# Where in the turn of the interaction stage the small product, the relu rows and the normalising stand

## The reference

```
h  = relu(layernorm(x))
hidden = silu(attr8 @ Wfc1 / sqrt(8));  w = (hidden @ Wfc2 / 8) as 4 x 32 for each edge
xs1, xv1 = (scalar and vector part of h[src]) * node_attr_input[src] @ w1 / sqrt(32)
m0, m3, m1, m2 = products of w, xs1 or xv1 and edge_attr (1 scalar, 3 vector parts)
mid = segment_sum([m0 m3 m1 m2], dst) / 4
x3 = x2 + node_attr_output * (mid @ w2) / sqrt(64)
h  = relu(layernorm(x3));  base = x3 + h + bu'
n  = normalise(h);  ndT = (n * ln_g + ln_b) transposed;  attention terms = wa.T @ ndT
```

## Time and profile before

| | |
|---|---|
| median of 3 runs | 4488.05 us (4477.16 to 4498.65) |
| profiled execution, its own time | 4457.76 us |
| its span in the trace | 4456.1 us |
| PE, DVE, ACT, POOL busy | 3021.5, 3403.5, 2148.5, 2108.6 us |
| mean granted clock of PE | 0.819 |

### The profile page before, as it was taken

How to read it: one execution, slowest core, us unless ns; L and a number is a source line. 1 busy time by engine, 2 the same in 40 slices (tenths; PEclk the granted TensorE clock), 3 DMA queues, 4 the chain that set the end, 5 groups by cost and what they waited for, 6 DMA issues and landing times. The chain is left out here.

```text
span 4456.1 us, 67687 instructions
## 1 busy us (share of the span) xinstructions
PE 3021.5 (68%) x12366; PEld 1720.8 (39%) x12366; DVE 3403.5 (76%) x10033; ACT 2148.5 (48%) x5598; POOL 2108.6 (47%) x2258
## 2 busy tenths in 40 slices
PE   5956644444445999478999124888888999506886
PEld 1255533333332444123444112555545666303443
DVE  6978868888886888675555785888885666597997
ACT  0057766677662222162222265676765666304554
POOL 0057767777775554006553002555545555103566
PEclk9977767777767999689999555898888999758998
DMA  2079966776672222174331596444445556303333
GB/s 51 2 209 285 285 219 219 231 232 227 225 219 87 65 62 59 45 222 86 62 62 42 135 246 157 121 125 121 126 107 180 194 195 199 112 0 110 114 112 87
DMA packets 622136, 627.73 MB, mean 141 GB/s; under 512 B 168453, under 2 KB 495711, under 8 KB 615589
## 3 DMA queue, kind: packets, MB, share of 16 engines
q1 hardware_dynamic: 574020, 523.79, 39.3%
q0 software_dynamic: 48000, 102.76, 9.4%
HBM read 333.97 MB, written 296.91 MB: 142 GB/s over the span
## 5 line engine op out<-in xcount | busy, mean ns | idle before, releaser
L1410 PE MATMUL r_pM<-r_masked,wr 128*128 128x512 f32 x1600 | 747.3, 620 | 55.2 <-DVE r_masked L1361 55.2
L1361 DVE SCALAR_TENSOR_TENSOR r_masked<-r_typ,r_hT 128x512 f32<-128x512 f32 x800 | 493.9, 688 | 238.4 <-ACT r_hT L1388 189.1
L1410 PEld LDWEIGHTS r_pM<-r_masked,wr 128*128 128x128 f32 x1600 | 307.7, 198 | 424.3 <-issue 293.2
L1252 PE MATMUL e_pY<-ident,e_agg 128*128 128x128 f32 x400 | 134.0, 438 | 367.6 <-DVE e_agg L1127 340.3
L741 POOL DMA_INDIRECT q_rows<-nr,row_x x200 | 258.8, 1294 | 193.3 <-PE q_pT L590 132.3
L2408 POOL DMA_INDIRECT out<-o_base,o_at_o x200 | 239.4, 1197 | 165.1 <-DVE o_base L2449 96.8
L741 POOL DMA_INDIRECT r_xs<-h_tab,r_at_s x200 | 214.8, 1074 | 87.7 <-issue 47.0
L741 POOL DMA_INDIRECT r_xs<-tab,r_at_s x200 | 212.4, 1062 | 89.1 <-issue 48.2
L1252 PEld LDWEIGHTS e_pY<-ident,e_agg 128*128 128x128 f32 x400 | 106.9, 327 | 379.5 <-issue 202.4
L590 PE MATMUL g_pT<-ident,g_hT 128*128 128x128 f32 x400 | 95.9, 384 | 226.7 <-ACT g_hT L1772 176.0
L1006 PE MATMUL na_pZ<-w,na_aT 128*128 128x128 f32 x784 | 158.9, 385 | 117.5 <-ACT na_aT L988 117.4
(11 more groups left out here) (402 smaller groups left out, 8958.4 us busy)
## 6 DMA issues: line engine op xcount, KB each, us to landing
xz<-na_xz SPq DMA_DIRECT2D x49, 1040.0 KB, 5.7
r_typ<-vec_s SPq DMA_DIRECT2D x100, 256.0 KB, 3.4
g_al<-alpha_s SPq DMA_DIRECT2D x100, 256.0 KB, 4.3
na_xz<-in_x SPq DMA_DIRECT2D x49, 512.0 KB, 7.0
tab<-na_x SPq DMA_DIRECT2D x49, 512.0 KB
e_xin<-tab SPq DMA_DIRECT2D x49, 512.0 KB, 6.4
hr<-e_hh SPq DMA_DIRECT2D x49, 512.0 KB, 3.8
zh_s<-e_zh SPq DMA_DIRECT2D x49, 512.0 KB, 4.5
```

The costliest lines, as they stand in the source:

```text
L1252: pe.matmul(pY[s][:, cols], agg[s][:, cols], g.ident[:, :], start=True, stop=False)
L1361: v.scalar_tensor_tensor(masked[:, r, :], typ[d.slot(4)][:, :], float(r), hT[d.slot(2)][:, :], ALU.is_equal, ALU.mult).then_inc(ev.mk, 1)
L1410: pe.matmul(pM[s][:, :], g.wr[:, layer * R_ + r, :], masked[:, r, :], start=(r == 0), stop=(r == R_ - 1)).then_inc(ev.mm, 1)
```

## The change

`line = Line(4, 10, 8)` gives one turn more. On DVE the small product and the normalising leave the end of the turn and stand behind the scan and hid, now for blocks t-5 and t-6. On ACT the relu rows leave the end of the turn and stand between the copies hT and ws, for block t-5. What follows n (PE's transposes, ndT, product with wa, attention terms, the stores) goes one turn later. Statistics, rz, rh and POOL's adds keep their lags.

```
-    line = Line(4, 10, 7)
+    line = Line(4, 10, 8)
 sync:
-                b = at(6)   # store of n, then of base
+                b = at(6)   # store of base
+                b = at(7)   # store of n
-                b = at(7)   # stores of ndT, att
+                b = at(8)
 vector, behind hid (L1916) and ahead of the messages:
+                b = at(5)
+                if b:
+                    v.wait_ge(ev.rz, b.now())
+                    v.wait_ge(ev.hh, b.back(1))
+                    v.scalar_tensor_tensor(nm[:, :], mv[:, :, 0], -1.0, rz[:, :], ALU.mult, ALU.mult).then_inc(ev.nm, 1)
+                d = at(6)
+                if d:
+                    s = d.slot(2)
+                    v.wait_ge(ev.rh, d.now())
+                    v.wait_ge(ev.ts, d.back(2))
+                    if d.k >= 2:
+                        v.wait_ge(w_n[s], 16 * d.uses(2))
+                    normalise(v, hh[s], mvh, rh, n_[s], ev.nn)
 vector, at the end of the turn: the same lines for at(4) and at(5) are removed
 scalar, behind hT (L1999) and ahead of ws (L2002):
+                d = at(5)
+                if d:
+                    s = d.slot(2)
+                    a.wait_ge(ev.nm, d.now())
+                    a.wait_ge(ev.nn, d.back(2))
+                    a.wait_ge(ev.ba, d.back(2))
+                    for j in range(J):
+                        last = a.activation(hh[s][:, j, :], x3[s][:, j, :], ACT.Relu, scale=rz[:, j:j + 1], bias=nm[:, j:j + 1])
+                    last.then_inc(ev.hh, 1)
 scalar, at the end of the turn: the same lines for at(4) are removed
 scalar: ndT and att, both at(6) -> at(7)
 tensor: f = at(6) -> f = at(7)
```

More of the change, by code:

```diff
@@ L1856, in turn @@
                     s = b.slot(2)
-                    wait_alone(g, sp, ev.nn, b.now())
-                    sp.dma_start(b.edge_rows(g.nr, N), n_[s][:, :, :]).then_inc(w_n[s], 16)
                     wait_alone(g, sp, ev.ba, b.now())
@@ L1861, in turn @@
                 b = at(7)
+                if b:
+                    s = b.slot(2)
+                    wait_alone(g, sp, ev.nn, b.now())
+                    sp.dma_start(b.edge_rows(g.nr, N), n_[s][:, :, :]).then_inc(w_n[s], 16)
+                b = at(8)
                 if b:
@@ L1961, in turn @@
                     stats(v, c, g, hh[d.slot(2)], sth, mvh, ev.sh)
[L1962 to L1972, removed]
             line.sweep(v, turn, c)
@@ L2009, in turn @@
                     a.activation(sg[:, :], sg[:, :], ACT.Exp, scale=-1.0).then_inc(ev.si, 1)
-                b = at(6)
+                b = at(7)
                 if b:
@@ L2033, in turn @@
                     rstd(a, g, c, mvh, rh, ev.rh)
[L2034 to L2041, removed]
             line.sweep(a, turn, c)
@@ L2048, in turn @@
             def turn(at):
-                f = at(6)
+                f = at(7)
                 if f:
```

## The result

After: 4465.79 us in the median (4457.16 to 4471.82, 12 runs). Before, on the same chip: 4484.11 us (4470.82 to 4498.65, 12 runs). The ratio is 0.9964 (95% interval 0.9952 to 0.9975), some 16 us: a small gain that this many runs can tell from nothing. The two medians differ by 18.3 us. The forecast was 4473 and 15 us.

The account below looks back on a forecast made before the run. Neither DVE nor PE is full; waits inside an interaction turn bound it, DVE ending full-clock turns, PE slow-clock ones. 41 turns x (11.74 - 11.38) = 15 us saved, plus 1, less 1, carried from 4488.05 to 4473 us; range 4448 to 4501.

Parts of the forecast that it names:

- Path of a turn: In the interaction stage: scan, hid, small product, normalising, products, pM, ACT, pL, 11.31 us a turn at full clock.
- The hold: A DVE instruction with both operands in SBUF stands until 1.12 us after a POOL add has begun.
- lower end of 10.64: The interaction turn with nothing in the way of the products: 10.64 us.
- Rival (a): POOL's adds don't meet DVE's products; turn 10.64 to 10.75 us, 42 us saved, 4446 us; chance 0.17.
- The hold to the end of the instruction: DVE's products stand until each POOL add ends: 11.65 us a turn, kernel within 3 us of before.
- rival c: No change at all: DVE held to each POOL instruction's end, or short clock falls not hidden; 4485 to 4489; chance 0.12.
- The clock: PE's long falls, which make 12.97 us turns, go; a short fall in one turn of three costs 0.07 us a turn.
- Every turn ends with pL: PE's product pL ends every new turn, as in the 18 turns with no fall behind them, so long falls should go.
- Rival (b): Clock keeps falling for long in at least every second turn; 4505 us at one half, 4538 in all; chance 0.13.
- new stand before pM: PE waits 1.5 us each turn for the last message product before its transposes into pM.
- Sum: Interaction stage: 15 us saved in 41 turns, 1 us in four turns before, 1 us lost at the end; 4473 us.
- The tail: Stage's end: 1 us lost, between 0 and 3, for DVE's small product and normalising ahead of the last x3.

Follow-up runs that it names:

- e1: Kernel after, with POOL's two additions per turn cut to two of 128 columns per tile: 4419.19 us, 0.9909 of before.
- e4: Kernel after, with POOL's two additions held until DVE has done the turn's last product: 4412.97 us, 0.9906 of before.
- e6: Kernel after, with normalising put between the products and x3, and POOL's additions held until it is done: 4401.47 us, 0.9874 of before.
- e3: Kernel after, with the relu rows and the small product put back at the turn's end, only normalising kept moved: 4502.39 us, 1.0099 of before.
- e7: Kernel before, with one unused PE product added each turn between pL and the product with hid: 4431.47 us, 0.9925 of before.
- e10: The e6 kernel, with DVE repeating four bn_stats at the turn's end into a spare tile: 4460.76 us, 0.9969 of before.
- e5: Kernel after, unchanged, run and profiled again: 4445.38 us, 0.9959 of before.

## Why the prediction was right, and where it wasn't

- **Path of a turn.** L1955 (L1939 before) was to be due at S+4.50: S+4.40. The hold was to end 1.12 us after POOL's start: 1.12 and 1.13. POOL's total was to start at S+3.94: S+3.78 to 4.01. The last product was to end at S+6.97: S+6.81 to 7.03. From there to pL's end 4.30 us: 2919.72 to 2924.03 is 4.31. The wait for pL before the scan was to be 0.4 us: 20.8 us in 42, 0.5. The turn at full clock, the loop's edge apart: 11.16 to 11.38, forecast 11.31. e1 and e4 confirm the term by taking it away (my lower end of 10.64: 10.55 at full clock). Rival (a) names that state, but nothing in after leads to it.
- **The hold to the end of the instruction** (11.65 us, rival c): the mean is 11.37, and the rows above show DVE through at 1.12 and 1.13 of 1.27 us.
- **The clock.** Long falls gone, a short one in every third turn: 0 and 13 of 41. A short one costs 0.1 to 0.2 us (11.35 for 11.16), 0.06 us a turn, forecast 0.07. The reason behind it was half right. "Every turn ends with pL" is not what keeps the clock up: e6's turns don't, and keep it; and e3's end with pL and fall. What PE does between pL and the next product matters: a product put in (e7) takes the long falls out of before, and 0.75 us more of the stretch (e10) brings them back. How it depends on the length stays open: 3.0 us once in four turns did nothing in e6. So does what else has a part in it (e3).
- **Rival (b)** had PE's new stand before pM bring the long falls back. At 1.2 to 1.4 us it doesn't; at 2.1 to 2.3 us in e3 a fall of 3.4 us began 0.4 to 1.2 us behind it in five of nine turns, and no longer one.
- **A term that was missing, and luck.** The loop's edge costs 0.28 us in nine of the 41 turns, 0.06 us a turn, and the forecast had nothing for it. The path of a full-clock turn was as much too long (11.25 us in the mean without the edge, forecast 11.31). The two cancel, and the mean of 11.37 for 11.38 is closer than the terms were.
- **Sum.** 41 turns: 15 us forecast, 15.2 measured undisturbed. Before them 1 us: 1.8 (from POOL's first instruction 97.8 us before, 96.0 after). The tail was mis-sized: 1 us lost was forecast, between 0 and 3, and it is 3.7 (41.4 us before, 45.1 after, from the last marked scan to the last store); the two turns up to the last scan take 12.2 and 13.1 us, for 10.8 and 12.1 before. 13.3 us in the stage. The two profiled times differ by 19.1, and 5.4 of that is ahead of the stage, in code that is the same.
- **What I didn't have:** PE's late semaphores, and that normalising can be held by POOL too. The second didn't touch the forecast, as normalising ends at S+2.95 and POOL starts at S+3.8; it made e3's expectation wrong by some 73 us (37 us less than before expected in the 41 turns, 517.61 - 481.23 = 36 more measured).

## What to carry to other kernels

Moving a step off one engine's end moves what waits for it: here relu's move brought POOL's additions from one victim to another, and one wait that holds them in the right place was worth more than the whole change (in the 41 turns 26.0 us, 466.07 - 440.04, against 15.2). Before crediting a new order, list every POOL instruction and what DVE does beside it, one-input instructions too. And read the granted clock turn by turn: where long and short turns alternate, look for the stretch in which PE has only transposes, and try to fill or shorten it: here both worked (e7, and e6 against e10).

## What the runs showed of the hardware that I had not expected

- Four tensor_scalar instructions of 128x128 fp32 from SBUF to SBUF, in a row, went from 1.10 to 3.07 us beside two POOL additions (e3).
- 0.61 us of useless product per turn made the kernel 35 us faster (e7).
- In 4 of 13 profiles PE's semaphores rose late, by up to 2.2 us behind the end shown in the first profile of after and 2.4 in e10, with different kernels (before and after among them), and the profile named a transfer that didn't run as what was waited for. What holds them back is open; the three that were taken on one of the chips all had it. POOL's late gathers, which I had suspected, don't: e5 has them where the first profile of after has, without it.
